# The last batch's slot list made by comparisons and products, and another filling of the second layer's double steps

## The reference

```python
x = x + _L0_attn_ref(_layernorm(x), wq, wk, wv, wo)          # 16 heads of 16, softmax(-arccosh distance)
x = x + _L0_ffn_ref(_layernorm(x), router_w, w_gate, w_up, w_down, ws_gate_up, ws_down)
x = x + _L1_attn_ref(_layernorm(x), Wq, Wkv_down, Wk_up, Wv_up, Wo)   # 8 heads of 64, latent of 64
x = x + _L1_ffn_ref(_layernorm(x), Wq, Wk, Ws, Wd, Wv, Wo)   # attention whose values are mixed from 5 experts
```

```python
topk_w, topk_ids = jax.lax.top_k(probs, K)                   # K = 8 of E = 64
onehot = flat_e[:, None] == jnp.arange(E)[None, :]
pos = jnp.cumsum(onehot, axis=0)[jnp.arange(N), flat_e] - 1  # place within the expert
valid = pos < C                                              # C = 128
x_buf = jnp.zeros((E * C + 1, x.shape[1]), x.dtype).at[idx].set(x[tok])
```

## Time and profile before

| | us |
|---|---|
| median of 3 runs | 2882.74 (2882.38 to 2884.28) |
| the profiled execution | 2907.69 |
| its span, first to last instruction | 2906.0 |
| mean granted clock of PE | 0.872 |

### The profile page before, as it was taken

The page is one execution under the profiler, slowest core; times in us unless marked ns, Lnnn a source line. Parts: engine busy times, 40 slices in busy tenths (PEclk is TensorE's granted clock), DMA queues, the critical chain, the costliest instruction groups (busy, mean ns, idle before and its releaser), DMA issues. The chain is left out here.

```text
span 2906.0 us, 31407 instructions
## 1 busy us (share of the span) xinstructions
PE 2383.2 (82%) x10131; PEld 1160.0 (40%) x10131; DVE 1873.5 (64%) x3109; ACT 1674.5 (58%) x2352; POOL 1923.5 (66%) x1920
## 2 busy tenths in 40 slices
PE   4677777777777777763989899999999999999886
PEld 2222323332323332321555454455555545454543
DVE  3788989888989888831333455555656565656545
ACT  0578888889788888950222354454545454545341
POOL 5456577877878787964677103948484858493876
PEclk8668787878787877785999999999999999999986
DMA  2000000000000000143997300001010000000000
GB/s 100 1 15 1 15 17 15 17 15 17 16 17 8 24 8 17 15 69 55 249 265 178 96 1 1 1 1 23 1 22 1 23 1 23 1 8 1 8 1 15
DMA packets 92450, 98.96 MB, mean 34 GB/s; under 512 B 20320, under 2 KB 88032, under 8 KB 92256
## 3 DMA queue, kind: packets, MB, share of 16 engines
q1 hardware_dynamic: 66544, 69.80, 8.9%
q0 software_dynamic: 25712, 26.90, 4.8%
HBM read 69.98 MB, written 26.67 MB: 33 GB/s over the span
## 5 line engine op out<-in xcount | busy, mean ns | idle before, releaser
L948 POOL TENSOR_TENSOR TT<-TT,SS 128x512 f32<-128x512 f32 x512 | 652.3, 1309 | 216.6 <-ACT SS L877 215.4
L1676 ACT ACTIVATE PR<-S,NM 128x512 f32<-128x512 f32 x512 | 344.9, 686 | 285.2 <-DVE NM L1843 285.2
L1843 DVE TENSOR_REDUCE NM<-S 128x2 f32<-128x1024 f32 x256 | 302.1, 1220 | 199.9 <-PE S L1570 199.9
L700 DVE TENSOR_SCALAR TT<-SC 128x1024 f32<-128x1024 f32 x256 | 311.7, 1217 | 74.5 <-POOL TT L948 45.4
L447 PE MATMUL OB<-TT,VAL 128*17 128x512 f32 x1024 | 340.3, 767 | 7.9 <-ACT TT L885 7.9
L953 POOL DMA_INDIRECT slot_tokens<-TID,IDX x256 | 258.6, 1010 | 130.3 <-issue 79.9
L702 DVE SCALAR_TENSOR_TENSOR SS<-SC,TT 128x1024 f32<-128x1024 f32 x256 | 313.6, 1225 | 20.6 <-issue 1.8
L1581 PE MATMUL TP<-ident,PR 128*128 128x128 f32 x2048 | 281.6, 281 | 25.0 <-DVE TT L1848 21.9
L1682 ACT ACTIVATE TT<-TP 128x512 f32<-128x512 f32 x256 | 153.2, 598 | 221.9 <-PE TP L1581 219.2
L1581 PEld LDWEIGHTS TP<-ident,PR 128*128 128x128 f32 x2048 | 233.3, 143 | 109.8 <-issue 63.4
L1848 DVE COPY TT<-TP 128x512 f32<-128x512 f32 x256 | 176.3, 689 | 148.2 <-PE TP L1581 145.4
(11 more groups left out here) (272 smaller groups left out, 4096.6 us busy)
## 6 DMA issues: line engine op xcount, KB each, us to landing
TT<-w_gu SPq DMA_DIRECT2D x64, 384.0 KB
TT<-w_dn SPq DMA_DIRECT2D x64, 128.0 KB
XL<-x SPq DMA_DIRECT2D x8, 512.0 KB
rows<-XL SPq DMA_DIRECT2D x8, 512.0 KB
slot_tokens<-TID,IDX POOLq DMA_INDIRECT x256
TT<-w_dn SPq DMA_DIRECT2D x64, 64.0 KB
XS<-stream SPq DMA_DIRECT2D x8, 512.0 KB, 4.0
out<-XS SPq DMA_DIRECT2D x8, 512.0 KB, 2.9
```

The lines of the kernel that those rows point to most:

```text
L700: dve.tensor_scalar(tt[:, :, mt, :], SC[mt % 2][:], 0.0, None, ALU.max)
L948: ins = pool.tensor_tensor(tt, tt, ss, ALU.add)
L1676: act.activation(PR[s % 2][h2][:], S[s % 2][:, h2, :], ACT.Exp, bias=NM[:, s % 2, h2:h2 + 1], accum_out=SM[:, pair % 2, j, h2:h2 + 1]).the ...
L1843: dve.tensor_reduce(NM[:, s % 2, :], S[s % 2][:], AX, ALU.max, negate=True).then_inc(sems["peak"], 1)
```

## The change

**The slot list.** The list of the last batch is no longer written to the table and read back. For each tile j of tokens and each pick k DVE compares the place of every token with 0..127 (PLACES) and its expert with 0..63 (MARKS, once times the token's number in the tile, once times j-4), in bf16. A product PLACES^T x MARKS summed over the 32 columns (j, k) gives a 128 x 128 result: its left half has, for place and expert, the token's number in its tile, its right half a multiple of the tile. `earlier` adds what the batches before had put into the table: that is read by SP in the cycle b=8 as soon as batch 6's scatters have landed (L325 after), turned by PE, and empty places are filled by a comparison with the counts. The list `ids` lies in SBUF before the stage ends. With this, the 32 scatters of batch 6 are all issued in the cycle b=8 at p=0, behind the last sums of roots and ahead of rstd; the weights of four experts are asked for as before and those of the other eight behind the read of the list; PE runs three idle products behind the counts of the last batch; hid is a task of its own.

**The filling.** The tables of stage three have other rows. The last piece of `choose` and the first two pairs of `mix_values` stand at d=6 instead of d=7; `NORM_1`'s `stats` at d=7 instead of d=3; two of the four `queries1` products go to the next run; `gates` stands in slot A; `spread` and `heads2` in slot Z instead of A.

```diff
-def slots_ahead(tasks):
-    slots = [t for t in tasks if t[2] == "slots"]
-    logits = [t for t in tasks if t[2] == "logits"]
-    rest = [t for t in tasks if t[2] not in ("slots", "logits")]
-    at = [t[2] for t in rest].index("gate_up")
-    return rest[:at] + [rest[at][:2] + t[2:] for t in logits + slots] + rest[at:]
-
-
-TO_DVE_LAST = slots_ahead(TO_DVE)
+LAST_ROUTING = ("logits", "slots", "weights", "gate_up", "hid")
+TO_DVE_LAST = [t for t in TO_DVE if t[2] not in LAST_ROUTING and t[0] < 6] + [
+    (5, "late", name, i, "before") for name, i in (
+        ("logits", 0), ("slots", 0), ("gate_up", 0), ("gate_up", 1), ("mark", 0), ("gate_up", 2), ("weights", 0), ("gate_up", 3),
+        ("mark", 1), ("earlier", 0), ("hid", 0), ("list_last", 0), ("mark", 2), ("mark", 3), ("earlier", 1))]
+TO_DVE_END = TO_DVE + [(1, "late", "list_last", 1, "before2")]
...
+SOON = 4
...
-                    for e in range(UN):
+                    for e in range(SOON):
...
+                if p == 5 and b == B:
+                    for i in range(LANES):
+                        sp.wait_ge(sems[f"scattered{i}"], 16 * NT * K // LANES * (B - 1))
+                    sp.dma_start(into[2], slot_list).then_inc(sems["slots_in"], 16)
+                    for e in range(SOON, UN):
+                        request(sp, sems, w, into, e)
...
-                for i in range(LANES):
-                    sp.wait_ge(sems[f"scattered{i}"], 16 * NT * K // LANES * B)
-                sp.dma_start(into[2], slot_list).then_inc(sems["slots_in"], 16)
...
+                if v.b == B:
+                    keep_clock(v, 3)
...
+            def earlier(v, i, par):
+                if i == 0:
+                    pe.wait_ge(sems["earlier"], 1)
+                    pe.transpose(SC[1][:, 1, 0:E], EARLIER, ident[0:E, 0:E]).then_inc(sems["turned"], 1)
+
+            def list_last(v, i, par):
+
+                for j in (2 * i, 2 * i + 1):
+                    pe.wait_ge(sems["marked"], j + 1)
+                    for k in range(K):
+                        ins = pe.matmul(SC[1][:, 0, 0:2 * E], PLACES[:, j, k, :], MARKS[:, j, k].rearrange("p a e -> p (a e)"),
+                                        start=((j, k) == (0, 0)), stop=((j, k) == (NT - 1, K - 1)))
+                if i:
+                    ins.then_inc(sems["listed"], 1)
...
+                if v.b == B:
+                    dve.tensor_copy(BEFORE, CNT[:])
...
+                if v.b == B:
+                    slots_apart()
+                    return
...
+            def slots_apart():
+
+                dve.tensor_scalar(K8F.bitcast(U32), K8F, -1.0, None, ALU.add)
+                dve.drain()
+                dve.tensor_scalar(EK.bitcast(U32), K8F.bitcast(U32), int(math.log2(CAP)), None, ALU.logical_shift_right)
+                dve.tensor_scalar(PK.bitcast(U32), K8F.bitcast(U32), CAP - 1, None, ALU.bitwise_and)
+                dve.drain()
+                dve.tensor_copy(EK, EK.bitcast(U32))
+                dve.tensor_copy(PK, PK.bitcast(U32))
+                dve.drain()
+
+            def mark(v, j, par):
+
+                if j == 0:
+                    dve.wait_ge(sems["w"], H0 * B)
+                    dve.wait_ge(sems["counted"], 1)
+                    dve.tensor_copy(count, count_i)
+                    dve.tensor_copy(own, own.bitcast(I32))
+                    dve.drain()
+                of_j = slice(K * j, K * j + K)
+                dve.tensor_tensor(PLACES[:, j], count.unsqueeze(1).to_broadcast([P, K, P]),
+                                  PK[:, of_j].unsqueeze(2).to_broadcast([P, K, P]), ALU.is_equal)
+                dve.tensor_tensor(MARKS[:, j, :, 1, :], count[:, 0:E].unsqueeze(1).to_broadcast([P, K, E]),
+                                  EK[:, of_j].unsqueeze(2).to_broadcast([P, K, E]), ALU.is_equal)
+                dve.drain()
+                dve.tensor_scalar(MARKS[:, j, :, 0, :], MARKS[:, j, :, 1, :], own, None, ALU.mult)
+                dve.drain()
+                dve.tensor_scalar(MARKS[:, j, :, 1, :], MARKS[:, j, :, 1, :], float(j - NT), None, ALU.mult)\
+                   .then_inc(sems["marked"], 1)
+
+            def earlier(v, i, par):
+
+                if i == 0:
+                    dve.wait_ge(sems["slots_in"], 16)
+                    dve.tensor_copy(EARLIER, experts_in(TT)[2]).then_inc(sems["earlier"], 1)
+                    return
+                dve.tensor_scalar(OPEN, CNT[:], own, own, ALU.is_le, ALU.mult)
+                dve.tensor_scalar(GONE, BEFORE, own, own, ALU.is_le, ALU.mult)
+                dve.drain()
+                dve.tensor_tensor(OPEN, OPEN, GONE, ALU.subtract)
+                dve.drain()
+                dve.wait_ge(sems["turned"], 1)
+                dve.tensor_tensor(OPEN, OPEN, SC[1][:, 1, 0:E], ALU.add)
+
+            def list_last(v, i, par):
+
+                if i == 0:
+                    return
+                dve.wait_ge(sems["listed"], 1)
+                dve.drain()
+                dve.scalar_tensor_tensor(OPEN, SC[1][:, 0, E:2 * E], float(P), OPEN, ALU.mult, ALU.add)
+                dve.drain()
+                dve.tensor_tensor(ids[:], SC[1][:, 0, 0:E], OPEN, ALU.add).then_inc(sems["idx"], 1)
...
+                if p == 0 and b == B:
+                    pool.iota(count_i, [[1, P]], base=0, channel_multiplier=0)
+                    pool.iota(own.bitcast(I32), [[0, 1]], base=0, channel_multiplier=1)
+                    pool.drain()
+                    pool.sem_inc(sems["counted"], 1)
+                if p == 0 and b == B:
+                    for c0 in range(0, NT * K, SCATTERS):
+                        scatter_of(v, c0)
+                elif p < PAIRS - 1 and 2 <= b < B:
                     scatter(v, SCATTERS * (p + 1))
-                if p == PAIRS - 1 and before:
-                    pool.wait_ge(sems["slots"], v.next("slots"))
-                    pool.sem_inc(sems["slots_seen"], 1)
-                    scatter(v, 0)
+                if p == PAIRS - 1 and 1 <= b < B - 1:
+                    scatter_of(v, 0)
...
-            pe.wait_ge(sems["slots_f"], 1)
-            pe.transpose(x_ps[1][:, 0:E], SF[:], ident[0:E, 0:E]).then_inc(sems["slots_t"], 1)
...
-            dve.wait_ge(sems["slots_in"], 16)
-            dve.tensor_copy(SF[:], SI).then_inc(sems["slots_f"], 1)
-            dve.wait_ge(sems["slots_t"], 1)
-            dve.tensor_copy(IDS[:], x_ps[1][:, 0:E]).then_inc(sems["idx"], 1)
...
-    (0, 7, D3, "choose", 6), (0, 7, D3, "mix_values", 0), (0, 7, D3, "mix_values", 1), (0, 7, D3, "mix_values", 2),
...
+    (0, 6, D3, "mix_values", 0), (0, 6, D3, "mix_values", 1), (0, 6, C3, "queries2", 1),
+    (0, 7, A, "keys2", 1), (0, 7, D3, "mix_values", 2), (0, 7, D3, "mix_values", 3), (0, 7, C3, "queries2", 2),
...
-NORM_1 = table((0, 3, D3, "stats", 0))
-NORM_1_LATE = table((0, 5, D3, "stats", 0))
+NORM_1 = table((0, 7, D3, "stats", 0))
+NORM_1_LATE = table((0, 6, D3, "stats", 0))
 PREP_1 = table(
-    (0, 3, Z, "turn_norm", 0), (0, 3, C3, "turn_norm", 1), (0, 4, Z, "latent", 0), (0, 4, C3, "queries1", 0),
-    (0, 5, A, "values1", 0), (0, 5, Z, "queries1", 1), (0, 5, C3, "queries1", 2), (0, 6, Z, "queries1", 3))
+    (0, 3, Z, "turn_norm", 0), (0, 3, C3, "turn_norm", 1), (0, 5, A, "latent", 0), (0, 6, A, "queries1", 0),
+    (0, 6, C3, "values1", 0), (0, 7, A, "queries1", 1), (1, 1, C3, "queries1", 2), (1, 2, A, "queries1", 3))
...
-    order = {p: n for n, p in enumerate(("product_out2", "set_down", "heads1"))}
+    order = {p: n for n, p in enumerate(("product_out2", "set_down", "heads1", "choose", "merge", "stats"))}
```

115 lines of the change are left out of this document (66 added, 49 removed).

## The result

| | before | after |
|---|---|---|
| median of the runs | 2883.51 us (2882.38 to 2886.86) | 2806.18 us (2804.97 to 2808.25) |
| ratio | | 0.9729, 95% interval 0.9715 to 0.9744 |
| the profiled execution's span | 2906.0 us | 2805.2 us |

A forecast was written before the change was run, and what follows sets the result against it. No engine was taken to bound everything: stage one passes work among ScalarE, DVE and POOL, stage three is bound by PE. Slot list -24 and filling -50 gave -74: 2834 us profiled, 2809 median, range 2788 to 2850.

The forecast's parts named there:

- Part 1: Slot list at stage one's end: without the last scatters, waits and read back, the first gather comes 24.2 us earlier.
- the late start of 4.12: Stage one's end: L788 on DVE waits 4.12 us during the weight load; should that vanish, the list brings -28.
- the 12.34 that heads the list of what goes: Stage one's end: DVE's copy L818 waits 12.34 us for scatters in flight, counted as going.
- marks 2 and 3: Stage one's end, DVE: 5.8 us, covered between L837's end and L842; without that cover they cost 5.8.
- Part 2: Filling of stage three: reordered tables take off 36 us of idle time and 14 of clock, together -50 us.
- Shifted, not shortened: Stage three's end: run 15's tail hangs on POOL and its table keeps WV's place, so its length stays.
- the three that were to show the forecast wrong: Gather after 1372, clock below 1.00 in more than three of runs 2 to 14, or XN still releasing PE.
- Half of part 2: Rival, stage three: new waits replace old ones, idle -22, clock -7, slot list's gain whole; 2830 us; chance 0.18.
- the change does nothing for the list: Rival, stage one: the list is ready no earlier, only the filling gains; 2833 us; chance 0.13, shared with a small list gain.
- The stall of the scatters: Rival, stage one: the 11 us stall strikes before rstd, list gain -13, 2822 us; chance 0.13, shared with no list gain.
- The slower case: Rival, stage three: XN stands behind POOL's mixing, slack 7; WV some 18 us late costs 80, 2889 us; chance 0.05.
- The shared port: Stage three: small DVE operations held up by POOL's mixing; nothing in the sum, though 18 of the 50 could go.

The follow-up runs named there:

- e1: The change's stage-one code with the old tables of stage three; 2885.51 us, ratio 0.9920 to the kernel before.
- the five: Five traces, the kernel before's among them, whose first sums of roots begin at 85.5 to 96.7 us and which have DVE or POOL starts 3 us or more late.
- run 15: A stretch of stage three, eight double steps of one attention, not an experiment; with all behind it 140.6 us in the kernel before.
- e10: The change with the two moved queries1 products put back into the run before; 2823.69 us, ratio 0.9789 to the kernel before.
- run 14: A stretch of stage three, eight double steps of one attention, not an experiment; 90 us in the kernel before.
- e4: The change with the weights of all twelve experts asked for early instead of four; 2825.80 us, ratio 0.9703 to the kernel before.
- e3: The change with the last batch's rstd behind 12 of batch 6's 32 scatters instead of all; 2813.68 us, ratio 0.9678 to the kernel before.
- e8: The change with the last piece of choose (WV) and the first two pairs' mixing back at d=7; 2874.33 us, ratio 0.9963 to the kernel before.
- run 5: A kind-1 stretch of stage three, eight double steps of one attention, not an experiment; 73 us in the change.

## Why the prediction was right, point by point

**Part 1**, -24.2 forecast, -24.0 in the traces, -25.6 by the medians for the part alone (-23 by its ratio). The sum was right, but two terms were off and met in the middle:

| | forecast | in the trace (before less 19.0) |
|---|---|---|
| rstd later by | 10.4 | 1295.05 - 1278.9 = 16.2 |
| the counts' sum, L815, later by | 10.4 | 1307.16 - 1296.15 = 11.0 |
| hid later by | 0.6 | 1322.10 - 1322.16 = -0.1 |
| first gather earlier by | 24.2 | 24.0 |

rstd was 5.8 later than said. From the end of the roots to the first scatter 7.9 us passed (1246.73 to 1254.62), where two iotas were priced at 0.2 each by their lengths and what follows them at nothing; the roots themselves ended 1.8 earlier than said. The counts' sum made up 5 of this: the late start of 4.12, which was kept in the sum and set as a bound below, did not come back. That two errors of 5 us met is luck. There is more of it: the 12.34 that heads the list of what goes is a wait behind the scatter that was 11.30 late, and both late starts belong to the kind of execution that was profiled. How much of them stands in the median of the kernel before is not known, for lack of a trace of the other kind; e1, whose medians bear the sum out, belongs to the five as well. A mark took 2.6 us from L877 to the end of L884 (2.9 said), and marks 2 and 3 were under the shared product, as said. The transfers fitted.

**Part 2**, -50 forecast, and -58 in the trace (1273.5 - 1215.2), of which 6 are the clock at the end and not the filling: -52.

| | forecast | in the trace |
|---|---|---|
| idle time of runs 2 to 14 | -36 | 12.5 - 47.6 = -35.1 |
| clock, (1 - clock) x length | -14 | 81 x 0.04 + 86 x 0.04 = 6.7 is left of 18: -11 |
| PE's busy time beyond the clock | 0 | 951.4 - 933.5 - 11.3 = -6.6 |
| runs 0 and 1 | 0 | 133.7 to 136.0: +2.3 |
| run 15 and what follows | 0 | 140.6 to 133.4: -7.2, of it 5.9 clock of the last 21 us |
| sum | -50 | -57.9, and -58.3 without the rounding of the stretches |

Idle time is what was said, and of the clock 11 for 14. The rest, the 6.6 of busy time, was not seen: e10 shows that there is room hidden in the busy column, and this is the likely place, though no run takes the 6.6 apart. Of the new waits, 12.5 us in all, 5.3 stand in run 3 and some 6 in run 14, and none in the pairs between; 7 had been set against them, spread out. Run 14 was to take 76 us and takes 86. XN no longer holds it, but three pieces of `choose` now stand at its d=6 (`PREP_2_LAST`), and DVE counts for 9 us, from 2656.01 on, ahead of the copy that PE waits for. From the timelines of DVE and PE:

```profile
2662.27 2.95 DVE L1921 TENSOR_TENSOR CN<-CN,CM 128x256 f32<-128x256 f32 x1
...
2666.03 1.97 PE L1679 MATMUL TP<-ident,PR 128*128 128x128 f32 x8 [5.65 <-DVE TT L1946]
```

"Shifted, not shortened" was right for run 15, but for about 1 us: e1 shows its 134.0 us with the old tables.

**The profiled execution** was to take 2834 us, on the ground that its steps are those of the median. It took 2806.97, 27 less. The 25 us by which the one before stood above its median were not common to both: against the trace after, 19 us lay at its start and 6 at its end. The median, 2806.18 for 2809, does not hang on this.

**The signs.** Of the three that were to show the forecast wrong, one came: XN still releases PE, once, for 5.3 us in run 3. The other two did not: the gather is at 1341.94 + 19.0 = 1361, and the clock is below 1.00 in two of runs 2 to 14 and not in more than three. Of the signs for it, kind-1 runs of 73 us came; rstd at 1308 (it was 1295.05 + 19.0 = 1314), run 14 near 76 and a wait for TP under 8 us (12.9, with 5.7 of it in run 14) did not.

**The rivals.** "Half of part 2" and "the change does nothing for the list" fall with the result. The stall of the scatters falls with e4 and with every trace of the new order: none of the 32 is late, not even in e1, e3 and e4, which have late starts elsewhere. The slower case named the right mechanism, XN on POOL behind mixing, but in the wrong run. It counted the slack of the kind-2 run, 7 us (5.0 in the trace after), and put the point from which it decides at a WV 18 us late. e8 has it at one double step, with the statistics at d=7: 52.8 us of waits and a clock of 0.94, and what is left of the gain is 0.4%. The chance of 0.05 rested on that slack. The trace of before could have told. In its run 5 the XN of the kind-1 run is there in the timelines of POOL and PE, behind a gate sum that ends just as the statistics do, and taken 1.0 us after it is ready:

```profile
2023.63 2.90 POOL L1977 TENSOR_TENSOR GO<-GO,GT 128x1280 f32<-128x1280 f32 x1
...
2027.85 4.83 POOL L1919 TENSOR_SCALAR XN<-XS,mvl,rstd1b 128x256 f32<-128x256 f32 x4 [0.18 <-issue]
...
2033.66 0.66 PE L1405 MATMUL BK<-ident,XN 128*128 128x128 f32 x4
```

**The shared port.** Nothing was put into the sum for small DVE operations beside POOL's mixing, and no run of the pairs has a wait of PE there. The view of one line gives the least, median and greatest length in ns, before and after:

```profile
L1744 DVE TENSOR_SCALAR var1b<-mvl x16: 170/630/1836, 1618.1 to 2721.0; 128x4 f32<-128x4 f32 x16
```

```profile
L1842 DVE TENSOR_SCALAR var1b<-mvl x16: 170/292/1501, 1576.0 to 2630.3; 128x4 f32<-128x4 f32 x16
```

The median fell from 0.63 to 0.29 us as half of these moved from gate sums of 2.9 us to mixing operations of 0.6 to 0.7. The Trainium skill (SBUF — State Buffer, section "Who interferes with whom") lets such an operation wait for a whole instruction of the other engine; by that the trace agrees: in 21 cases of the two traces in which one runs beside an instruction of POOL, it ends 0.02 to 0.03 us after that one. So the move made these operations shorter, where it had been held against the change; PE's waits show nothing of it.

## What to carry to other kernels

Where a filling is changed in several places at once, look for the piece that the others lean on: the slack of every consumer of the moved result has to be read, not that of the nearest one, and in a pipeline over two kinds of run both have it. When a long row of issues is put in front of one small instruction on the same queue, ask who waits for the small one. A sum that comes out right can hide two wrong terms; only the timeline of the chain tells. And before two traces are subtracted, look whether the stretches that the change leaves alone are equal: here they were not, by 19 us at the start and 6 at the end.
